# Moving a decision from the middle of an attention kernel into its tail, and splitting the last output store over two queues

## The reference

```python
def _L0_attn_ref(in_features, q_proj, k_proj, v_proj, o_proj):
    # 16 heads of 16
    Q, K, V = (proj(q_proj), proj(k_proj), proj(v_proj))
    scores = jnp.einsum('bhqd,bhkd->bhqk', Q, K) / math.sqrt(d_k)
    scores = jnp.where(causal, -jnp.inf, scores)
    attn = jax.nn.softmax(scores, axis=-1)
...
    base = x_flat @ W.T + b
    logits = x_flat @ gate_w.T + gate_b
    topk_logits, topk_idx = jax.lax.top_k(logits, K)          # K = 2 of 8 experts
    gates = jax.nn.softmax(topk_logits, axis=-1)
    xA = jnp.einsum('nd,erd->ner', x_flat, lora_A)
    delta_all = jnp.einsum('ner,eor->neo', xA, lora_B)
...
x = x + attention(layernorm(x));  x = x + ffn(layernorm(x))
```

## Time and profile before

| | us |
|---|---|
| three executions | 330.9, 330.92, 333.09 |
| their median | 330.92 |
| the profiled execution, measured time | 332.83 |
| the profiled execution, span from its first to its last instruction | 330.9 |

### The profile page before, as it was taken

The page is one execution under the profiler, slowest core; times in us unless marked ns, Lnnn a source line. Parts: engine busy times, 40 slices in busy tenths (PEclk is TensorE's granted clock), DMA queues, the critical chain, the costliest instruction groups (busy, mean ns, idle before and its releaser), DMA issues.

```text
span 330.9 us, 8638 instructions
## 1 busy us (share of the span) xinstructions
PE 314.3 (95%) x3478; PEld 119.1 (36%) x3478; DVE 190.2 (57%) x613; ACT 273.9 (83%) x306; POOL 72.6 (22%) x99
## 2 busy tenths in 40 slices
PE   7999989999999999999999999997999999999794
PEld 2453434434434343334432333232223323322272
DVE  5627796576667627466164773583566456611752
ACT  2377799998999999999999999996899999999110
POOL 6377102222221302213021311130220322100000
PEclk9999999999999999999999999997999999999978
DMA  6567684101172102000139000000000000000001
GB/s 202 164 171 214 201 217 112 34 2 34 30 195 66 35 3 50 2 16 12 23 73 232 2 18 18 0 18 1 18 3 16 18 2 16 19 18 1 2 2 66
DMA packets 18986, 19.23 MB, mean 58 GB/s; under 512 B 10368, under 2 KB 15744, under 8 KB 18944
## 3 DMA queue, kind: packets, MB, share of 16 engines
q1 hardware_dynamic: 18848, 18.52, 21.0%
q10 hardware_dynamic: 96, 0.13, 0.2%
HBM read 12.35 MB, written 6.29 MB: 56 GB/s over the span
## 4 chain that ended last, share of the span: by engine, by line
PE 73%; ACT 10%; issue 6%; DVE 4%; DMA 3%; SPq 2%; POOL 0%; ACTq 0%
PE acc L940 28%; PE aux L768 18%; PE scores L923 17%; ACT probs L1067 10%; PE scores L768 4%; DMA x_sb<-x 2%; PE aux L810 1%; DMA k_stack<-k_dram 1%; DVE probs L1276 1%; PE aux L761 1%; DMA q_dram<-q_stack 1%; PE aux L823 1%; PE scores L855 1%; PE aux L868 1%; SPq L545 1%
## 5 line engine op out<-in xcount | busy, mean ns | idle before, releaser
L1067 ACT ACTIVATE probs<-scores 128x1024 f32<-128x1024 f32 x272 | 257.4, 1030 | 21.2 <-PE scores L923 19.5
L940 PE MATMUL acc<-probs,v_aug 128*32 128x512 f32 (+3 forms) x1280 | 136.5, 534 | 2.3 <-DVE turned L1282 1.6
L923 PE MATMUL scores<-q_stack,k_stack 64*128 64x512 f16 (+3 forms) x640 | 80.0, 350 | 4.8 <-ACT probs L1067 3.1
L1276 DVE TENSOR_TENSOR probs<-probs,mask_sb 128x512 f32<-128x512 f32 (+1 forms) x80 | 51.7, 677 | 26.6 <-ACT probs L1067 26.5
L923 PEld LDWEIGHTS scores<-q_stack,k_stack 64*128 64x128 f16 x640 | 22.9, 94 | 97.6 <-ACT probs L1067 82.0
L940 PEld LDWEIGHTS acc<-probs,v_aug 128*32 128x32 f32 x1280 | 37.0, 109 | 50.6 <-issue 31.9
L1580 POOL TENSOR_TENSOR rstd<-ve,minus_half 128x1 f32<-128x1 f32 x12 | 7.1, 589 | 69.1 <-DVE ve L1311 69.1
L1585 POOL TENSOR_TENSOR exp_gap<-euler,top_gap 128x1 f32<-128x1 f32 x12 | 7.4, 613 | 57.5 <-DVE top_gap L1337 53.0
L1327 DVE COPY ffn<-aux 128x392 f32<-128x392 f32 x12 | 6.8, 564 | 22.3 <-PE aux L768 22.3
L768 PE MATMUL aux<-wffn_sb,yT 128*32 128x392 f32 x192 | 18.3, 498 | 0.0
L1282 DVE STREAM_TRANSPOSE turned<-acc 128x512 f32<-128x512 f32 (+1 forms) x17 | 11.6, 680 | 9.8 <-PE acc L940 9.8
(11 more groups left out here) (163 smaller groups left out, 286.3 us busy)
## 6 DMA issues: line engine op xcount, KB each, us to landing
q_stack<-q_dram SPq DMA_DIRECT2D x14, 256.0 KB, 4.0
k_stack<-k_dram SPq DMA_DIRECT2D x28, 128.0 KB, 3.8
x_sb<-x SPq DMA_DIRECT2D x3, 512.0 KB, 5.6
out<-ffn SPq DMA_DIRECT2D x12, 128.0 KB, 1.7
q_dram<-parts SPq DMA_DIRECT2D x16, 64.0 KB, 2.2
k_dram<-parts SPq DMA_DIRECT2D x8, 128.0 KB, 2.2
wqkv_sb<-wqkv SPq DMA_DIRECT2D x3, 256.0 KB, 4.2
x_sb<-x SPq DMA_DIRECT2D x2, 256.0 KB, 3.1
```

The lines of the kernel that those rows point to most:

```text
L923: m = pe.matmul(scores[bank_of(u)][:, j, col:col + n], k_stack[row:row + STACK, kb // TPC, 2 * i + p, kb % TPC * P:(kb % TPC + 1) * P], q_ ...
L940: m = pe.matmul(acc[32 * hp:32 * hp + 32, lo:CHUNK], v_aug[:, kb, QUAD * i + hp, :], probs[:, u % PROBS, hp % 2, col:col + CHUNK - lo], st ...
L1067: act.activation(probs[:, u % PROBS], scores[bank_of(u)][:], ACT.Exp, scale=EXP_SCALE).then_inc(exp_done, 1)
L1276: dve.tensor_tensor(tile, tile, mask, ALU.min).then_inc(causal_done, 1)
```

## The change

Two things change. The call of `decide_bound` moves out of `read_norms` and behind the last `last_normalise` in VectorE's queue. And the last pair of tiles is added tile by tile: `last_finish` takes a slice of tiles and the number of pairs it waits for; tile 2 of the tail is stored from ScalarE's queue and tile 3 from SyncE's, each 128 KB. The first pair is stored as before. The final waits count three stores instead of two.

```diff
-            for p in range(2):
-                sp.wait_ge(last_result_ready, p + 1)
-                at = TILES - TPC + 2 * p
-                sp.dma_start(out[at:at + 2].rearrange("n p d -> p n d"), last_result[:, pair_of(p), :]
-                             ).then_inc(last_result_out, 16)
+            sp.wait_ge(last_result_ready, 1)
+            at = TILES - TPC
+            sp.dma_start(out[at:at + 2].rearrange("n p d -> p n d"), last_result[:, 0:2, :]).then_inc(last_result_out, 16)
+            sp.wait_ge(last_result_ready, 3)
+            sp.dma_start(out[TILES - 1], last_result[:, 3, :]).then_inc(last_result_out, 16)
...
-            sp.wait_ge(last_result_out, 16 * 2)
+            sp.wait_ge(last_result_out, 16 * 3)
...
+            act.wait_ge(last_result_ready, 2)
+            act.dma_start(out[TILES - 2], last_result[:, 2, :]).then_inc(last_result_out, 16)
+
...
                 dve.tensor_reduce(norms[:, c:c + 1], aux[0:64], AX_X, ALU.max).then_inc(norm_read, 1)
-                if c == NCHUNK - 1:
-                    decide_bound()
...
-            def last_finish(p):
-                dve.wait_ge(last_out_psum, p + 1)
-                dve.tensor_tensor(last_result[:, pair_of(p), :], y_banks[p].rearrange("p (n d) -> p n d", n=2),
-                                  biases_sb[:, 0:D].unsqueeze(1).to_broadcast([P, 2, D]), ALU.add
+            def last_finish(tiles, pairs):
+                dve.wait_ge(last_out_psum, pairs)
+                n, at = tiles.stop - tiles.start, tiles.start % 2
+                bank_of_pair = y_banks[tiles.start // 2].rearrange("p (n d) -> p n d", n=2)
+                dve.tensor_tensor(last_result[:, tiles, :], bank_of_pair[:, at:at + n, :],
+                                  biases_sb[:, 0:D].unsqueeze(1).to_broadcast([P, n, D]), ALU.add
                                   ).then_inc(last_result_ready, 1)
...
             for t in range(TPC):
                 last_normalise(t)
+
+            decide_bound()
             for p in range(2):
                 last_top_two(p)
             last_gates_of_all()
-            for p in range(2):
-                last_finish(p)
+            last_finish(slice(0, 2), 1)
+            for t in (2, 3):
+                last_finish(slice(t, t + 1), 2)
```

## The result

| | before | after |
|---|---|---|
| median of 20 executions, us | 331.11 | 329.29 |
| lowest and highest, us | 329.56, 333.09 | 327.74, 330.95 |
| ratio, 95% interval | | 0.9947 (0.993 to 0.9964) |
| profiled execution: time and span, us | 332.83, 330.9 | 330.56, 328.6 |

The forecast was 328.7 in a range of 326.6 to 330.0; 329.29 was measured. In both kernels some 1.9 to 2.0 us lie around the span.

A forecast was written before the change was run, and what follows sets the result against it. TensorE, busy 95%, was taken as the bound, its waits paid twice through the clock. Middle 2.98, tail 0 and stores 0.8 gave 3.8 us off the profiled execution, 329.0; the median reading gave 328.7, the forecast, range 326.6 to 330.0.

The forecast's parts named there:

- The middle: Slice 28: removing the decision before the turning saves 1.46 us of stall and 1.52 of slow clock, together 2.98.
- The check that ScalarE doesn't bind: Middle: ScalarE's exponentials are done in time, its wait of 2.90 us falling to about 0.4, then 0.26 idle.
- The reading of the median: Executions at 330.92 us had one slow stretch only; lacking the middle one, they save 2.26 and come to 328.7.
- The other way to the forecast: Whole kernel: the profiled execution, measured at 332.83 us, loses 3.8 and comes to 329.0.
- The stores: End: separate last stores gain 0.8 us, bounds -0.4 to 1.7; 0.4 with long issue and late DMA engine kept.
- the price of a single tile: End: a 128 KB store takes 0.33 us to issue and 1.7 to land, 3.8 at worst.
- Rival B: End: the stores give nothing, same bytes over the same 16 DMA engines; time 329.5 us, chance 0.10.
- The tail: The decision's 1.46 us fit into VectorE's 2.79 us wait for the ranks and cost nothing, over 1 us left.
- The 0.4 us I kept as a bound: Tail: without the slow stretch, ranks come some 1.7 us earlier and up to 0.4 of the decision sticks out.
- A: Middle or tail: one slow stretch fewer than counted; time 327.2 us, chance 0.34.
- C: Middle: it gives nothing because TensorE then waits for exponentials; time 330.1 us, chance 0.04.
- D: Behind 224 us: shifted work gets new slow stretches; one leaves 330.4 us, more are slower than before; chance 0.04.

The follow-up runs named there:

- experiment 2: Kernel after with the decision back in the middle, so only the last pair's adds and stores change; 331.45 against 331.29 us, ratio 1.0007.
- experiment 1: Kernel before with only the decision moved to the tail, behind the last normalisation, stores unchanged; 329.63 against 331.29 us, ratio 0.9954.
- experiment 3: Kernel before with the decision kept in the middle but behind the turning of acc; 329.48 against 331.29 us, ratio 0.9952.
- experiment 9: Kernel before with 14 matmuls that add no result filling TensorE's wait in the tail; 330.23 against 331.68 us, ratio 0.9959.
- experiment 7: Kernel after with the decision worked out twice in the tail; 329.84 us, ratio 0.9967 to the kernel before.
- experiment 5: Kernel after with 14 matmuls that add no result filling TensorE's wait in the tail; 328.67 us, against 331.12 of the kernel before, ratio 0.9919.
- experiment 10: Kernel before with both TensorE stalls filled by matmuls that add no result, 13 in the middle and 14 in the tail; 330.02 us, ratio 0.995.
- experiment 12: Kernel before with decision in the tail, tail wait filled, last pair stored whole from ScalarE's queue; 328.17 against 331.68 us, ratio 0.9891.

## Why the prediction was right, and where it was off

*The middle.* Right in place and size; of the mechanism the stall is shown, while the slow stretch behind it is a matter of chance. The stall of 1.46 us gave 1.50 (distance from norms to the group of 16: 2.94 against 1.44). The slow stretch was put at 1.52 us in the profiled execution; together 2.98 were forecast and 3.09 measured, which leaves 1.59 for the slow stretch, as experiment 2 has it. Experiments 1 and 3 show that the place in front of the turning cost it all. That the clock would not fall behind a stall of 0.16 us came out in this trace, but experiment 2's clock didn't fall behind one of 1.63 us either. The check that ScalarE doesn't bind held with 0.37 and 0.19 us of idle time, where 0.42 and 0.26 were worked out.

*The reading of the median.* The step that saved the forecast from the profiled execution's larger gain was that the median's executions had one slow stretch only. The clocks show that: the middle group of before, 0.991 to 0.993, has spans of 329.3 in the mean, which is 331.1 us of time. By experiment 9 at least two thirds of executions lack the middle stretch; which one the median executions had is not recorded. With the stores at their measured 0.2 the same reading gives 1.46 + 0.2 = 1.7 us off the median, and 1.8 was measured. In the mean over executions the middle stretch is worth up to a third of 1.7, some 0.6 us. The sum would then be 1.5 + 0.6 + 0.2 = 2.3 us, at the end of the interval of 1.2 to 2.3; that the difference is chance in the number of slow stretches is my guess. The other way to the forecast, the profiled execution, was forecast 3.8 us shorter and is 2.3 us shorter (332.83, 330.56): 1.1 of the difference is the later start, which no step foresaw, the rest the stores and the tail. Of the two ways to the forecast this one missed; the one by the median held.

*The stores.* The term was mis-sized: 0.8 us put, some 0.2 found, at most the 0.4 that the prediction had for its case with the long issue and the late DMA engine kept. The step that failed is the price of a single tile, 1.7 us to landing. It was read from stores that were alone in their queue. Tile 3 took 2.9 us (3.3 in experiment 7), where 2.3 was named as the sign. Behind the store of the first pair, beside the fetch of instructions, the issue takes 0.8 to 1.2 us instead of 0.33, as long as for the whole pair, and the late DMA engine stayed. A store ends with 16 landings. In the seven kernels with pairs on one queue the last landing of the last pair came 0.25 to 0.76 us after the fifteenth. That of the first pair came 0.74 to 1.06 us after, always 0.26 to 0.31 less than the fetch beside it took, which fits one of the 16 engines doing the fetch first; beside the last pair runs a second, shorter fetch, of 8 KB. The issue from ScalarE's queue took 0.39 us, where 0.65 to 0.72 was put. The trail after the bulk shows in the slices of the window 324 to 329 of the kernel after (each 0.125 us):

```profile
GB/s 0 0 0 0 0 131 0 0 0 0 172 336 360 319 319 360 295 344 377 156 33 320 336 303 115 25 41 25 16 8 0 0 0 0 0 0 0 0 0 0
```

After 115 GB/s come five slices at 8 to 41. Halving the last store shortened only the bulk. Rival B, nothing from the stores, is nearer to the times than my 0.8, and the rows stand between.

*The tail.* The decision cost nothing, as put. (Its end by the sum is 316.14 + 1.46 = 317.60, not 317.65.) The cover is thinner than the 2.8 us that the trace of before showed, because part of that was the slow clock: at full clock 0.26 us are left behind the decision, in experiments 1 and 5. So the sign that over 1 us of wait is left holds only in an execution with the slow stretch. The 0.4 us I kept as a bound did not come due, since the ranks come 1.15 us earlier at the full clock and not 1.7.

*The rivals.* A, one slow stretch fewer, is what 6 of 20 executions after do; their spans of 326.4 us are 328.2 of time, where A put 327.2 with the larger term for the stores. C and D are out: no stall was made up elsewhere, and the kernel after has fewer slow stretches, not more. D's ground, that a stall of this length can be followed by a slow stretch, is right.

## What to carry to other kernels

Read what stands in front of a read that frees a buffer: a small chain of instructions that nobody needs yet costs its full length there, and nothing a few instructions later. A wait of the busiest engine can be paid twice, once as idle time and once as slower work behind it, so look at the granted clock after each wait; and since that second payment comes in only some executions, count them over many executions before taking it from one profile. The price of a store read where its queue was empty is not its price behind another. Where an issue takes long, look first for a fetch of instructions beside it, and compare it with issues of the same size elsewhere.

## What the runs showed of the hardware

- The same program shows no, one or two slow stretches of TensorE, 1.15 in the mean of before's 91 executions; each lasts 3.4 us at half the clock. A stall of 1.6 us was followed by one in at most 4 of 12 executions (experiment 9), and of the three traces with it one has none (experiment 2). The wait of 1.82 us in the tail was followed by one in 9 of the 10 traces that have it. Where neither that stall nor an unfilled wait in the tail was left (experiments 5, 10 and 12), 23 of 25 executions had none at all. The Trainium skill (TensorE: Matmul & The Clock Gate, What's actually happening) says that the monitor's count is not tied to the kernel's start; these shares agree with it.
- A second issue on SyncE's queue behind a store of 256 KB ended 1.7 to 2.2 us after the first had begun, in twelve kernels, whether it began 0.6 or 0.9 us after it and whether it was 128 or 256 KB. In each it ended 0.38 to 0.43 us after a fetch of 16 KB of instructions, which took 0.96 to 1.42 us. On ScalarE's queue, in the same place and beside the same fetch, it took 0.39 to 0.44 us, with nothing ahead in that queue.
- Beside such a fetch one of a store's 16 landings comes late, by 0.74 to 1.06 us in the first pair's store of seven kernels.
- The start of the kernel differs by up to 1.6 us between executions of unchanged code (first exponential at 21.1 to 22.7 us), and 1.12 us of the difference between the two profiled executions is of this kind. The two latest, at 22.7, are the traces with a slow stretch at the start.
